# First expert products in split f16, denominators by half as many columns, one transpose and six expert products moved, a residual addition on GpSimd

## Chip, cores and metric

The kernel runs on one core of one Trainium2 chip, as one program. The metric is the device time of one execution in microseconds (us); a kernel is given as the median of its executions. TensorE (matrix products; PE in the profile, PEld its weight loads), VectorE (DVE), ScalarE (ACT), GpSimd (POOL) and the DMA queue of SyncE (SP) run side by side, each through its own list of instructions, and wait for one another on semaphores.

## What is computed

Two layers over x (16 batches, 56 rows, 128 wide). Each layer is a cross attention to a context of 1500 keys per batch, then a mixture of 8 experts of which each row takes 2. Both are scaled by tanh of a gain and added to x. Layer 1 has a key mask and a shared expert. The reference, shortened:

```python
def xattn(q_in, ctx, mask):            # H = 16 heads of 8
    q, k, v = heads(q_in @ Wq + bq), heads(ctx @ Wk + bk), heads(ctx @ Wv + bv)
    w = softmax(where(mask == 0, -1e9, q @ k.T / sqrt(8)))   # layer 0: no mask
    return join(w @ v) @ Wo + bo
def ffn0(x):                           # layer 0: 8 experts, 128 -> 512 -> 128
    p = softmax(x @ gate_w); top2 = top_k(p, 2), divided by their sum
    h = gelu(x @ w1[e] + b1[e]); y = h @ w2[e] + b2[e]
    return sum over the two of share * y
def ffn1(x):                           # layer 1: sigmoid gate, 128 -> 64 -> 128, and a shared expert
    ...
x = x + tanh(g_xattn[l]) * xattn(layernorm(x), ctx, mask)
x = x + tanh(g_ffn[l]) * ffn(layernorm(x))
```

## The kernel before

Everything is f32 unless it is said otherwise. A "batch" n is one of 32 (layer, batch) pairs; two batches side by side (T = 112 rows) form a group, for which queries, attention output and experts are computed together. The program is a software pipeline written out by hand: steps s = -1 to 35, each of 12 sub-steps kt = 0 to 11. Step s works on several batches at once:

- keys of batch s + 1 and values of batch s are projected (`project`, L1265 and L1274; f16 operands, each split in a high and a low part, three products);
- TensorE computes scores of batch s once to find their maxima (`max_scores`, L1229, two chunks of 500 keys in each sub-step, into the two halves of pMX; VectorE reduces each in `largest`, L1072). The next chunk but one waits for that reduction;
- scores of batch s - 1 (from sub-step 3) and s - 2 (up to sub-step 2) are computed again, shifted by the maximum (`score_half`, L1187), ScalarE takes the exponential (L789), and every other sub-step (the even ones) TensorE multiplies by the values (`weigh`, L1208, f32, into pO);
- odd steps from 3 have the first part of the experts of a group (`has_a`), even steps from 4 the second (`has_f`), odd steps from 5 the end (`has_end`).

The order of the small pieces within a step stands in tables: `kv_uses` (the projections in pKV), `fh_uses` (buffer pFH) and `fy_uses` (buffer pFY). An entry (kt, name, n) says that TensorE does the piece at the end of sub-step kt, and VectorE reads the result at the start of the next. pFH and pFY are single buffers: each piece waits until VectorE has read the one before it (`free`). The maximum reductions of a sub-step stand behind those reads in VectorE's list.

The names that matter here:

- **h0 to h7** in pFH (L1399): first product of expert e of layer 0, 4 f32 matmuls of 128x128 by 112 columns (each two instructions in the trace). VectorE adds the bias and writes HR (`hidden`, L970), ScalarE applies Gelu in sub-step 9 of the even step (L798). h0, h1 are at sub-steps 10, 11 of the odd step, h2 to h7 at 0 to 5 of the even one. There are 8 such groups, with their even steps 4 to 18; in steps 16 and 18 the attention is already that of layer 1.
- **ct** in pFY (L1306): the maxima (`m`, then `cc`, L1082 to L1087) are transposed and copied to ct (L1010), from where SyncE sends them as two shift rows into qexp (L546). `score_half` of batch s - 1 waits for that DMA at sub-step 3.
- **sum** (L1287): VectorE masks pO into OM (L1098), both heads of a pair in columns of their own (224); a product with sel gives the denominators, VectorE takes the reciprocal rden (L1014), GpSimd multiplies OM by it (L688) and adds the value bias into ON (L689). **y** (L1293) is the output projection, 4 f32 matmuls.
- **xT** (L1297, L1027): normalized rows of the group, transposed, in f32 as xnfT. **y0 to y3**: second expert products (L1328 and L1332), weighted by the shares in VectorE (L1043), added up on GpSimd (L709 to L714). **yb** (L1039): the expert biases and the residual input.
- VectorE ends the group in sub-step 11 of the odd step: X = acc1 * gain + acc0 (L1122). In its list, the maxima m and cc of the next step come right behind it.
- GpSimd splits the next context into Chi and Clo (L730, L732), and the keys into khi and klo (L641, L643).

In layer 0 the maximum products and the scores use different row halves of TensorE's array, and run side by side (`together`); in layer 1 they use all rows (`apart_`).

## Time and profile before

| | us |
|---|---|
| median of three runs | 1011.62 (1010.51 to 1013.26) |
| the profiled execution: its time | 1013.23 |
| the profiled execution: its span | 1011.4 |
| TensorE busy | 899.4 (89%), mean granted clock 0.97 |
| VectorE busy | 730.1 (72%) |
| ScalarE busy | 588.1 (58%) |
| GpSimd busy | 516.9 (51%) |

The page of the profile gives busy times, the span in 40 slices, the chain that ended last and the costliest groups of instructions. The view by line groups the instructions of a line by shape: count, busy time, mean ns, and what ended the idle time before them. The view in order of time shows start, duration, engine and line, with the idle time in brackets. Durations of matmuls contain their latency: what one costs in a stream is read from the start of the next.

### The profile page before, as it was taken

The numbers are of one execution on the slowest core, as the hardware profiler recorded it, in microseconds if no ns is written. First come the engines' busy times: TensorE is split into PE (matmuls) and PEld (weight loads), VectorE is DVE, ScalarE is ACT, GpSimd is POOL, SyncE is SP. The second block draws the span as 40 slices with busy tenths as digits, with TensorE's granted clock in tenths as the row PEclk, the third lists the DMA queues.
The fourth block names the chain that finished last, engine by engine and source line by source line (L and its number), as shares of the span: only waits on it lengthen the run. The fifth ranks groups of instructions, "written<-read, shape, count | busy, mean of one in ns | idle before, by whom it ended". The sixth has DMA issues, their size and how long they took to land.

```text
span 1011.4 us, 32583 instructions
## 1 busy us (share of the span) xinstructions
PE 899.4 (89%) x13088; PEld 651.2 (64%) x13088; DVE 730.1 (72%) x1576; ACT 588.1 (58%) x1077; POOL 516.9 (51%) x662
## 2 busy tenths in 40 slices
PE   3888998989899898988999999999999899999975
PEld 1355676766767676776767776666666666666754
DVE  5675876868678587786867858777787778787723
ACT  2155666575755757557475575757666575757560
POOL 5544554545445354553555456676666576662211
PEclk9978999999999999999999999999999999999995
DMA  6245432212222122222656656676766656675200
GB/s 158 77 123 150 129 112 92 80 49 73 70 84 78 51 68 72 80 79 67 119 116 127 138 96 142 137 156 127 156 148 121 140 124 143 137 137 99 55 2 19
DMA packets 103554, 104.47 MB, mean 103 GB/s; under 512 B 28442, under 2 KB 97388, under 8 KB 103404
## 3 DMA queue, kind: packets, MB, share of 16 engines
q1 hardware_dynamic: 101986, 102.07, 43.3%
q8 instruction: 104, 1.70, 0.8%
q10 hardware_dynamic: 1418, 0.32, 0.2%
q14 instruction: 46, 0.38, 0.1%
HBM read 35.89 MB, written 0.46 MB: 36 GB/s over the span
## 4 chain that ended last, share of the span: by engine, by line
PE 58%; DVE 25%; ACT 9%; issue 6%; DMA 1%; ACTq 1%; SPq 0%; DVEq 0%
DVE mx L1072 14%; PE pO L1208 13%; PE pMX L1229 10%; PE pST L1187 8%; PE pKV L1274 6%; PE pKV L1265 6%; PE pFH L1399 5%; PE pFY L1328 3%; ACT P L789 2%; DVE rden L1014 2%; ACT HR L798 2%; DVE HR L970 2%; ACT L789 2%; PE pFY L1332 2%; DVE ysc L1043 1%
## 5 line engine op out<-in xcount | busy, mean ns | idle before, releaser
L1072 DVE TENSOR_REDUCE mx<-pMX 112x1 f32<-112x500 f32 x768 | 487.4, 668 | 127.9 <-PE pMX L1229 125.0
L789 ACT ACTIVATE P<-pST 125x448 f32<-125x448 f32 x768 | 389.6, 542 | 277.7 <-PE pST L1187 272.4
L1229 PE MATMUL pMX<-kop,qmax 48*112 48x500 f16 (+1 forms) x768 | 284.3, 408 | 50.1 <-DVE mx L1072 37.3
L1187 PE MATMUL pST<-qexp,kop 50*128 50x112 f16 (+2 forms) x3072 | 266.7, 215 | 13.0 <-ACT P L789 7.9
L1187 PEld LDWEIGHTS pST<-qexp,kop 50*128 50x128 f16 (+2 forms) x3072 | 183.7, 100 | 78.0 <-issue 23.8
L1208 PE MATMUL pO<-P,V 125*17 125x112 f32 x6144 | 188.5, 264 | 0.0
L1229 PEld LDWEIGHTS pMX<-kop,qmax 48*112 48x112 f16 (+1 forms) x768 | 97.4, 129 | 124.0 <-DVE mx L1072 57.6
L1208 PEld LDWEIGHTS pO<-P,V 125*17 125x17 f32 x6144 | 138.1, 98 | 35.0 <-issue 18.7
L641 POOL CAST khi<-kfull 128x500 f16<-128x500 f32 x96 | 57.7, 601 | 190.1 <-ACT kfull L816 188.6
L643 POOL TENSOR_TENSOR klo<-kfull,khi 128x500 f16<-128x500 f32 x96 | 108.8, 1134 | 7.8
L732 POOL TENSOR_TENSOR Clo<-C,Chi 128x500 f16<-128x500 f32 x93 | 105.7, 1137 | 7.5
L821 ACT ACTIVATE V<-pKV 125x512 f32<-125x512 f32 x96 | 57.0, 594 | 36.9 <-PE pKV L1274 32.8
L688 POOL TENSOR_TENSOR OM<-OM,rden 128x224 f32<-128x224 f32 x32 | 21.0, 657 | 106.7 <-DVE rden L1014 106.7
L1399 PE MATMUL pFH<-xnfT,w1a 128*128 128x112 f32 x512 | 70.9, 281 | 5.0 <-DVE HR L970 4.9
L816 ACT ACTIVATE kfull<-pKV,bkp 128x500 f32<-128x500 f32 x48 | 32.5, 677 | 69.2 <-PE pKV L1265 65.9
L1274 PE MATMUL pKV<-Whi,Chi 128*128 128x128 f16 (+1 forms) x384 | 72.1, 225 | 0.5
L1274 PE MATMUL pKV<-Whi,Clo 128*128 128x128 f16 (+1 forms) x384 | 71.4, 223 | 0.4 <-issue 0.4
L1274 PE MATMUL pKV<-Wlo,Chi 128*128 128x128 f16 (+1 forms) x384 | 71.4, 223 | 0.0
L1399 PEld LDWEIGHTS pFH<-xnfT,w1a 128*128 128x128 f32 x512 | 63.6, 191 | 11.3 <-DVE HR L970 8.9
L1043 DVE TENSOR_TENSOR ysc<-pFY,gate 112x512 f32<-112x512 f32 x32 | 22.1, 691 | 61.5 <-PE pFY L1328 45.0
L730 POOL CAST Chi<-C 128x500 f16<-128x500 f32 x93 | 56.5, 607 | 17.6 <-PE pKV L1274 14.7
L1328 PE MATMUL pFY<-w2a,HR 128*112 128x128 f32 x512 | 61.1, 275 | 3.6 <-ACT HR L798 3.6
(151 smaller groups left out, 1106.8 us busy)
## 6 DMA issues: line engine op xcount, KB each, us to landing
C<-in_ctxT SPq DMA_DIRECT2D x31, 750.0 KB, 6.7
kop<-maskop SPq DMA_DIRECT2D x48, 437.5 KB
kop<-khi SPq DMA_DIRECT2D x192, 62.5 KB
kop<-khi SPq DMA_DIRECT2D x96, 125.0 KB
kop<-klo SPq DMA_DIRECT2D x96, 62.5 KB
kop<-klo SPq DMA_DIRECT2D x48, 125.0 KB
maskin<-in_mask SPq DMA_DIRECT2D x8, 656.2 KB, 5.5
qexp<-qmax SPq DMA_DIRECT2D x16, 182.0 KB
```

The source lines that it names most:

```text
L641: nc.gpsimd.tensor_copy(khi[:, cols], kfull[:, c, :]).then_inc(khi_done, 1)
L643: nc.gpsimd.tensor_tensor(klo[:, cols], kfull[:, c, :], khi[:, cols], ALU.subtract).then_inc(klo_done, 1)
L732: nc.gpsimd.tensor_tensor(Clo[:, s % 2, cols], C[:, cols], Chi[:, s % 2, cols], ALU.subtract).then_inc(ctx_split, 1)
L789: nc.scalar.activation(P[0:KP, slot, h * 4 * T:(h + 1) * 4 * T], pST[0:KP, h, 0:4 * T], ACT.Exp, scale=EXP_SCALE).then_inc(exp_done, 1)
L1072: nc.vector.tensor_reduce(mx[:, s % 2, c, p:p + 1], pMX[0:T, m % 2, 0:CW], AX.X, ALU.max).then_inc(max_done, 1)
L1187: mm = nc.tensor.matmul(pST[0:keys.stop - keys.start, h, i * T:(i + 1) * T], kop[rows, b, slot, keys], qexp[rows, b, slot, :, :].rearrange ...
L1208: mm = nc.tensor.matmul(pO[32 * g:32 * g + VW, r * T:(r + 1) * T], V[0:KP, b, tile, p, :], P[0:KP, tile % RING, p * T:(p + 1) * T], start= ...
L1229: nc.tensor.matmul(pMX[0:T, m % 2, 0:CW], qmax[rows, b, slot, :, :].rearrange("r j q -> r (j q)"), kop[rows, b, slot, c * CW:(c + 1) * CW] ...
L1265: mm = nc.tensor.matmul(pKV[:, 0:CW], m[:, l, 0, :], x_[:, b, cols], start=(i == 0), stop=(i == 2))
L1274: mm = nc.tensor.matmul(pKV[0:rows, i * D:(i + 1) * D], x_[:, s % 2, cols], m[:, l, 1, :], start=(k == 0), stop=(k == 2))
L1328: mm = nc.tensor.matmul(o, HR[:, F0C * e + c, :], w2a[:, e, c, :], start=(c == 0), stop=(c == F0C - 1))
L1399: mm = nc.tensor.matmul(pFH[:, c * T:(c + 1) * T], w1a[:, e, c * 128:(c + 1) * 128], xnfT[:, :], start=True, stop=True)
```

## The change

1. w1 of layer 0 is kept as two f16 tensors w1hi and w1lo, and xT also writes f16 parts xfhi and xflo. Each f32 product of h0 to h7 becomes three f16 products (hi hi, hi lo, lo hi). The raw weights pass through the buffer HR. ScalarE makes w1hi (8 copies in steps 2 and 3), GpSimd w1lo (8 subtractions), and one of the eight loads moves from step 2 to step 3.
2. Masking pO becomes two instructions that bring both heads of a pair into the same 112 columns of OM. V has one more column of ones. The products of sum, the reciprocal, and OM and ON on GpSimd have half as many columns, and y has two matmuls instead of four. The tensors bvm and the wide headmask go away.
3. ct is transposed in the middle of sub-step 1, behind the first half of the scores, instead of at the end of sub-step 0; VectorE copies it between the two maxima of sub-step 1.
4. h2 to h7 are at sub-steps 0, 1, 2, 3, 6, 7 instead of 0 to 5.
5. X is made on GpSimd in two instructions (multiply, add) behind its sums, in all groups but the last.

The diff, cut to its core:

```diff
-VW = PR + 1
+VW = PR + 2
@@ fh_uses / fy_uses
-        uses += [(e - 2, f"h{e}", 1) for e in range(2, 8)]
+        uses += [(k, f"h{e}", 1) for e, k in zip(range(2, 8), (0, 1, 2, 3, 6, 7))]
-        uses.append((0, "ct", 1))
+        uses.append((1, "ct", 1))
@@ SyncE, expert_weights
-                if s in (1, 2):
-                    for e in range(4 * (s - 1), 4 * s):
-                        sp.dma_start(w1a[:, e, :], w1_0[e]).then_inc(w1_in[e // 2], 16)
+                if s in (1, 2, 3):
+                    for e in range(4 * (s - 1), min(4 * s, E0 - 1)) if s < 3 else (E0 - 1,):
+                        if e == E0 - 1:
+                            sp.wait_ge(w1_split, 1)
+                        sp.dma_start(w1raw[:, raw_columns(e)], w1_0[e]).then_inc(w1_in[e], 16)
@@ GpSimd
+            def expert_low(st, i):
+                if st.s in (2, 3):
+                    e = 4 * (st.s - 2) + i
+                    pool.wait_ge(w1_hi, e + 1)
+                    nc.gpsimd.tensor_tensor(w1lo[:, e, :], w1raw[:, raw_columns(e)], w1hi[:, e, :], ALU.subtract
+                                            ).then_inc(w1_split, 1)
                 low_part(st, 0)
+                expert_low(st, 0)
...
                 low_part(st, 1)
+                expert_low(st, 1)
...
                 low_part(st, 2)
+                expert_low(st, 2)
+                expert_low(st, 3)
...
                     nc.gpsimd.tensor_tensor(acc[:, 1, :], ysc[:, 0, 0, :], ysc[:, 0, 1, :], ALU.add).then_inc(ysum_done, 1)
+                    pool.wait_ge(ysum_done, end_count(s) + 1)
+                    link(nc.gpsimd.tensor_scalar(acc[:, 1, :], acc[:, 1, :], gains[0:T, g:g + 1], None, ALU.mult))
+                    pool.wait_ge(fy_free, upto(fy_uses, s, "yb", True))
+                    nc.gpsimd.tensor_tensor(xg((s - 5) // 2), acc[:, 1, :], acc[:, 0, :], ALU.add).then_inc(x_done, 1)
@@ ScalarE
+                    if s in (2, 3) and kt in (1, 3, 5, 7):
+                        e = 4 * (s - 2) + kt // 2
+                        act.wait_ge(w1_in[e], 16)
+                        nc.scalar.activation(w1hi[:, e, :], w1raw[:, raw_columns(e)], ACT.Copy).then_inc(w1_hi, 1)
@@ VectorE
-                        nc.vector.reciprocal(rden[:, :], pFY[:, 0:2 * T]).then_inc(fy_free, 1)
+                        nc.vector.reciprocal(rden[:, :], pFY[:, 0:T]).then_inc(fy_free, 1)
-                        nc.vector.tensor_copy(xnfT[:, :], pFY[:, 0:T]).then_inc(fy_free, 1)
+                        if l == 0:
+                            link(nc.vector.tensor_copy(xnfT[:, :], pFY[:, 0:T]))
+                            link(nc.vector.tensor_copy(xfhi[:, :], pFY[:, 0:T]))
+                            nc.vector.tensor_tensor(xflo[:, :], pFY[:, 0:T], xfhi[:, :], ALU.subtract).then_inc(fy_free, 1)
+                        else:
+                            nc.vector.tensor_copy(xnfT[:, :], pFY[:, 0:T]).then_inc(fy_free, 1)
-                        nc.vector.tensor_tensor(OM[:, s % 2, :], pO[:, 0:2 * T],
-                                                headmask[:, :, :, :].rearrange("p r j q -> p (r j q)"),
-                                                ALU.mult).then_inc(o_free, 1)
+                        link(nc.vector.tensor_scalar(om, of[:, 0], headmask[:, 0:1], None, ALU.mult))
+                        nc.vector.scalar_tensor_tensor(out=om, in0=of[:, 1], scalar=headmask[:, 1:2], in1=om,
+                                                       op0=ALU.mult, op1=ALU.add).then_inc(o_free, 1)
+                    if kt == 1 and has_m(s - 1):
+                        from_fy(0, "ct")
-                    if has_end(s) and kt == 11:
-                        if not ends(s):
-                            dve.wait_ge(ysum_done, end_count(s) + 1)
+                    if ends(s) and kt == 11:
@@ TensorE
-                        mm = nc.tensor.matmul(pFY[:, 0:2 * T], sel[:, :], OM[:, s % 2, :], start=True, stop=True)
+                        mm = nc.tensor.matmul(pFY[:, 0:T], sel[:, :], OM[:, s % 2, :], start=True, stop=True)
-                            for j in range(2):
-                                mm = nc.tensor.matmul(pFY[0:T, 0:D], ON[:, r, j, :, :].rearrange("p b q -> p (b q)"), woE[:, l, r, :],
-                                                      start=(r == 0 and j == 0), stop=(r == 1 and j == 1))
+                            mm = nc.tensor.matmul(pFY[0:T, 0:D], ON[:, r, :, :].rearrange("p b q -> p (b q)"), woE[:, l, r, :],
+                                                  start=(r == 0), stop=(r == 1))
                             score_half(st, kt, h)
+                            if kt == 1 and h == 0 and has_m(s - 1):
+                                small("ct")
...
                         score_half(st, kt, 0)
+                        if kt == 1 and has_m(s - 1):
+                            small("ct")
-                                    mm = nc.tensor.matmul(pFH[:, c * T:(c + 1) * T], w1a[:, e, c * 128:(c + 1) * 128],
-                                                          xnfT[:, :], start=True, stop=True)
+                                    for i, (w1, x_) in enumerate(((w1hi, xfhi), (w1hi, xflo), (w1lo, xfhi))):
+                                        mm = nc.tensor.matmul(pFH[:, c * T:(c + 1) * T], w1[:, e, c * 128:(c + 1) * 128],
+                                                              x_[:, :], start=(i == 0), stop=(i == 2))
```

## Rows read from the trace of the kernel before

**Rows 1.** The page: busy time, share of the span and instructions of each engine.

```profile
PE 899.4 (89%) x13088; PEld 651.2 (64%) x13088; DVE 730.1 (72%) x1576; ACT 588.1 (58%) x1077; POOL 516.9 (51%) x662
```

**Rows 2.** Stretch, length, PE PEld DVE ACT POOL busy, granted clock, DMA share, GB/s.

```profile
216.73:278.33 61.60, 55.71 (x872) 43.31 (x869) 46.09 (x98) 37.32 (x68) 29.18 (x39) 1.00 0.22 70
480.00:600.00 120.00, 115.17 (x1619) 86.24 (x1611) 86.74 (x183) 72.06 (x128) 66.49 (x78) 1.00 0.62 119
764.00:766.00 2.00, 2.00 (x32) 1.34 (x25) 0.84 (x3) 0.41 (x1) 1.21 (x2) 0.50 1.04 134
```

**Rows 3.** By line and shape: count, busy us, mean ns, idle time before them.

```profile
L1399 PE MATMUL pFH<-xnfT,w1a 128*128 128x112 f32 x512 | 70.9, 281 | 5.0 <-DVE HR L970 4.9
L1274 PEld LDWEIGHTS pKV<-Whi,Clo 128*128 128x128 f16 (+1 forms) x384 | 39.6, 103 | 0.0
L1014 DVE RECIPROCAL rden<-pFY 128x224 f32<-128x224 f32 x32 | 49.4, 1544 | 2.2 <-PE pFY L1287 2.2
L1054 DVE RECIPROCAL g<-g 112x8 f32<-112x8 f32 x8 | 1.6, 203 | 0.3
```

**Rows 4.** TensorE in order of time, step 8 (layer 0).

```profile
249.15 1.15 PE L1399 MATMUL pFH<-xnfT,w1a 128*128 128x112 f32 x8 [0.23 <-DVE HR L970]
250.22 0.42 PE L1229 MATMUL pMX<-kop,qmax 48*112 48x500 f16 x1
254.20 1.04 PE L1399 MATMUL pFH<-xnfT,w1a 128*128 128x112 f32 x8
255.17 0.41 PE L1229 MATMUL pMX<-kop,qmax 48*112 48x500 f16 x1
```

**Rows 5.** TensorE in order of time: first and last of twelve f16 value products.

```profile
300.75 0.23 PE L1274 MATMUL pKV<-Whi,Chi 128*128 128x128 f16 x1
...
301.38 0.22 PE L1274 MATMUL pKV<-Whi,Clo 128*128 128x128 f16 x1
```

**Rows 6.** VectorE in order of time, end of step 7 and start of step 8.

```profile
245.05 0.62 DVE L970 TENSOR_TENSOR HR<-pFH,W 128x448 f32<-128x448 f32 x1 [0.43 <-PE pFH L1399]
246.76 1.11 DVE L1122 SCALAR_TENSOR_TENSOR X<-acc,gains 112x128 f32<-112x128 f32 x1
247.79 0.17 DVE L1082 TENSOR_REDUCE m<-mx 112x8 f32<-112x24 f32 x1
248.00 0.36 DVE L1086 TENSOR_SCALAR cc<-m 112x8 f16<-112x8 f32 x1
252.26 0.63 DVE L970 TENSOR_TENSOR HR<-pFH,W 128x448 f32<-128x448 f32 x1
```

**Rows 7.** GpSimd in order of time, same place as rows 6.

```profile
246.59 1.14 POOL L732 TENSOR_TENSOR Clo<-C,Chi 128x500 f16<-128x500 f32 x1
```

**Rows 8.** VectorE in order of time, steps 3 and 4, where no X is made.

```profile
122.73 0.62 DVE L970 TENSOR_TENSOR HR<-pFH,W 128x448 f32<-128x448 f32 x1 [0.43 <-PE pFH L1399]
129.07 0.62 DVE L970 TENSOR_TENSOR HR<-pFH,W 128x448 f32<-128x448 f32 x1
```

**Rows 9.** Both engines in order of time, step 7, sub-steps 1 and 5.

```profile
219.64 1.24 DVE L1072 TENSOR_REDUCE mx<-pMX 112x1 f32<-112x500 f32 x2
220.00 2.00 PE L1328 MATMUL pFY<-w2a,HR 128*112 128x128 f32 x16
231.10 0.37 DVE L1098 TENSOR_TENSOR OM<-pO,headmask 128x224 f32<-128x224 f32 x1
235.39 0.70 DVE L996 TENSOR_SCALAR qhi<-pFH,head_of 128x112 f16<-128x112 f32 x2 [0.17 <-PE pFH L1390]
```

**Rows 10.** VectorE in order of time, layer 1, the same place as rows 6.

```profile
793.61 0.69 DVE L1122 SCALAR_TENSOR_TENSOR X<-acc,gains 112x128 f32<-112x128 f32 x1
794.42 0.97 DVE L1086 TENSOR_SCALAR cc<-m 112x8 f16<-112x8 f32 x1
```

**Rows 11.** The chain that ended last, in order of time: start, us, what.

```profile
980.81 1.57 DVE rden L1014
986.67 2.06 PE pFY L1293 x8
```

More of the change, by code:

```diff
@@ L217, in links @@
         n += 2
+    if is_batch(s - 2):
+        n += 1
     if has_q(s):
@@ L365, in build @@
         xnfT = sb("xnfT", [128, T])
-        ones = xnfT
+        xfhi, xflo = sb("xfhi", [128, T], F16), sb("xflo", [128, T], F16)
         lg = sb("lg", [T, NE])
@@ L392, in build @@
         w_in, x_in, f_in, f2_in, wo_in = sem("w_in"), sem("x_in"), sem("f_in"), sem("f2_in"), sem("wo_in")
-        w1_in, w2_in = [sem(f"w1_in{i}") for i in range(4)], [sem(f"w2_in{i}") for i in range(4)]
+        w1_in, w2_in = [sem(f"w1_in{i}") for i in range(E0)], [sem(f"w2_in{i}") for i in range(4)]
         c_in = sem("c_in")
@@ L427, in build @@
         gelu_done = sem("gelu_done")
+        w1_hi, w1_split = sem("w1_hi"), sem("w1_split")
         x_done = sem("x_done")
@@ L930, in output_biases @@
                 dve.wait_ge(init_a, 1)
-                dve.wait_ge(init_l, 7)
-                for j in range(2):
-                    for l in range(LAYERS):
-                        for r in range(2):
-                            nc.vector.tensor_scalar(bvm[:, l, r, j, :], ones[:, 0:S], rowmask[:, j:j + 1],
-                                                    bvE[:, l, r:r + 1], ALU.mult, ALU.mult).then_inc(init_l, 1)
+                dve.wait_ge(init_l, 6)
                 for l in range(LAYERS):
@@ L1042, in from_fy @@
                         k = int(use[1]) // 2
+                        if k == 0 and end_count(s - back):
+                            dve.wait_ge(ysum_done, end_count(s - back))
                         nc.vector.tensor_tensor(ysc[:, k, :, :], pFY[0:T, 0:4 * D].rearrange("t (e d) -> t e d", e=4),
@@ L1077, in step @@
                 for kt in range(KT):
+                    if s == 3 and kt == 11:
+                        dve.wait_ge(w1_split, E0)
                     if s == 1 and kt == 8:
@@ L1370, in step @@
                         score_half(st, kt, 1)
-                    for use in [u[1] for u in fy_uses(s) if u[0] == kt and not early(u[1])]:
+                    for use in [u[1] for u in fy_uses(s) if u[0] == kt and u[1] != "ct" and not early(u[1])]:
                         small(use)
```

65 lines of the change are left out of this document (37 added, 28 removed).

## The prediction

> **What bounds the kernel now.** I read the engines' shares first: TensorE is busy 89% of the span, VectorE 72% [rows 1]. A share is a mean, so I went on to busy time by stretch [rows 2]: a pair of steps of layer 0 takes 61.60 us with TensorE busy for 55.71, steps 16 to 18 have it busy for 115.17 of 120.00, and layer 1 for 326.29 of 350.00. TensorE sets the pace, but not everywhere. The order of time shows where VectorE does: in the light sub-steps (no `weigh`, no projection) it has two maxima (1.17 us from start to start) and the bias of one expert (0.54 us), and TensorE waits for it before the next expert, 0.23 us in the row of 249.15 [rows 4]. From h0's bias at 245.05 to h3's at 252.26 VectorE is busy nearly throughout [rows 6]. In heavy sub-steps TensorE is late and VectorE idles. So a shorter TensorE piece counts in full in a heavy sub-step and hardly in a light one, and a shorter VectorE piece the other way round.
>
> **The change part by part.** I make the sum per kind of step, by walking both engines through the twelve sub-steps with the durations of the rows.
>
> *Expert products.* One expert costs 1.07 us from its start to the next maximum's after a wait and 0.97 us in a stream [rows 4]. As f16 it is twelve products of 112 columns. The nearest rows are the value products, f16 with 128 columns: 0.63 us for eleven intervals, 0.057 us each [rows 5]. Twelve are 0.68 us at that rate and 0.60 if the time goes with the columns; I take 0.65. One expert saves 0.3 to 0.45 us, I take 0.38, and 64 experts take 24 us off TensorE.
>
> *X off VectorE.* It holds VectorE for 1.03 us at 246.76 (to the start of m at 247.79) [rows 6]. Steps 3 and 4, which make no X, show its worth in the old kernel: from h0's bias to h3's take 6.34 us there and 7.21 us in step 7 [rows 6, 8], so 0.87 us. But it is long because GpSimd runs at the same time: it ends when Clo (246.59 + 1.14) ends [rows 7], and cc, 0.36 us here, takes 0.97 us in layer 1 [rows 6, 10]. Without X, cc comes earlier, into the stream of Chi and Clo, which the two new GpSimd instructions (about 1.3 us) push later. I charge 0.3 us; the bounds are 0 and 0.8. The Trainium skill (GPSIMD Engine Reference, Specifications) says that GpSimd shares its SBUF interfaces with VectorE, with contention for VectorE instructions in a 2-port mode or with two SBUF inputs; the trace agrees, as X and cc are the ones that stretch.
>
> *Even step of layer 0.* From h0's bias to sub-step 2: X gone -1.03, h0 and h1 sooner -0.35, the rest of the experts' saving hidden behind VectorE, ct no longer waiting for cc -0.55, cc in contention +0.3: -1.65. Sub-steps 2 to 7: h4 and h5 leave their places and h6 and h7 come to 6 and 7, where VectorE has time since rden shrinks. rden is 1.54 us for 224 columns and 0.20 for 8 [rows 3], so 0.85 for 112: -0.70. TensorE now paces this stretch: four experts -1.4 and the half sum product -0.2, against +0.35 for the masking in two instructions and +0.2 for tighter waits on the single buffer: -1.05. Together -2.7 (bounds -1.5 and -4.0, the latter eight experts at 0.38 and X in full). The later ct still has time: its DMA is issued at sub-step 1 and needed at 3.
>
> Steps 6, 8, 10, 12, 14: 5 x 2.7 = 13.5. Step 4 has no X to lose: 2.7 - 1.0 = 1.7. Steps 16 and 18 are TensorE's nearly alone [rows 2]: eight experts at 0.38 and part of X and rden, 3.5 each, 7.0.
>
> *Odd steps get longer.* (a) y2 is now behind ct in the single buffer pFY, so it waits for VectorE's copy, which stands between the maxima of sub-step 1. Those start at 219.64, y2 at 220.00 [rows 9]; the copy would end at 220.35. That is +0.35, and nothing behind y2 takes it back, since TensorE is late there. (b) The masking of pO takes two instructions. The nearest pair, also linked by a wait, is qhi, 0.70 us for two [rows 9], against 0.30 from OM's start to the next maximum's: +0.35, and sum and both maxima of sub-step 5 stand behind it. (c) Half the sum product gives back 0.1. The reciprocal and y give nothing, since from qhi at 235.39 [rows 9] up to xT VectorE has no gap, and rden lies ahead of that, beside TensorE's heavy sub-step. xT's two further instructions (0.65 us) lie in sub-step 10, where VectorE idled for 0.76 us; if that cover went, they would cost up to 0.65. So +0.6 in each of 7 steps (5 to 17): +4.2.
>
> *Layer 1.* Even steps: X and the wait for cc -0.6, rden on VectorE's run behind sum -0.7, masking +0.35, half a sum product -0.05: -1.0, 6 times (20 to 30), -6.0. Odd steps, 19 to 31: +0.45 as above, 7 times, +3.2. y saves 0.5 us of TensorE, but the next maximum waits for VectorE there.
>
> *Start.* ScalarE's 8 copies (some 0.6 us) and GpSimd's 8 subtractions (1.13 us, as klo) lie in steps 2 and 3. Behind GpSimd's last two stand xnf and the context split of step 3. SyncE's new wait for w1_split is over a step before; behind it stand the context load and the key DMAs. I take +1.0 (bounds 0 and +4). Masking twice +0.7, rden in step 2 -0.7: +1.0 in all.
>
> *End.* rden, 1.57 us, and y, 2.06 us at half the clock, lie bare on the chain [rows 11]: -0.7 and -1.0. Masking +0.35, sum -0.2, and ct later by 0.45 in step 32, where its DMA was waited for: -1.1.
>
> Sum: +1.0 - 1.7 - 13.5 - 7.0 + 4.2 - 6.0 + 3.2 - 1.1 = -20.9 us. On the profiled execution, 1013.23 us with a span of 1011.4, that is 992.3; the median of the runs, 1011.62, is 1.6 lower than that execution, so **990.7, say 991 us**.
>
> **The rivals.** *TensorE alone decides* (B): all 24 us of the experts count, with X at 0.87 in 13 steps (11), rden and y as above (8), and the odd steps' charges are half absorbed (-4): about -36, **976 us**. For it speaks the 89% of rows 1, against it the wait in rows 4.
>
> *VectorE and GpSimd get in each other's way* (C): cc and X's successors cost the upper bound, 0.8, not 0.3, in 13 steps (+6.5), and the light sub-steps hide more (1.0 less in each of 6 even steps, +6): -8.4, **1003 us**, range 998 to 1010. For it speaks the 0.97 us of rows 10.
>
> *The clock falls* (D), a case on the other side: layer 0's TensorE has 55.71 busy in 61.60 us at the full granted clock, 1.00 [rows 2]; the change takes about 4 us of work from it and 2 us from the time. In layer 1 there is a stretch at 0.50, the lower level (1.2 GHz), from 764 on [rows 2]. If 3 us of TensorE's work run at half the clock, they take 1.5 us more. From 14 such stretches on, one for each step of layer 0 from 4 on, the gain is gone: 991 + 21 = **1012 us**. Against it: the pair of layer 0 leaves TensorE idle a tenth of the time already, and stays at 1.00 throughout.
>
> *The f16 products don't stream* (E), slower: their f16 weight load lasts 103 ns [rows 3]. If each product waited for its own, an expert would take 12 x 0.103 = 1.24 us instead of 1.07 at most: +0.17 x 64 = +11, in place of the 15 us that experts give in the sum (1.5 in each of 6 steps, 3.0 in each of 2): -20.9 + 15 + 11 = +5, **1017 us**. It decides from 0.09 us a product. Rows 5 speak against it, 0.057 us with the same loads. The Trainium skill (TensorE: Matmul & The Clock Gate, Back-to-back issue gap) gives about 81 ns for a product of 128 columns in a stream of loads and products; by that an expert would take 0.97 us and save nothing in a stream. The trace disagrees at 57 ns.
>
> **How the numbers follow.** Forecast 0.52, B 0.12, C 0.26, D 0.06, E 0.04. The forecast's own bounds are 984 to 998. The range, 978 to 1004, takes in C's middle and the near side of B and leaves out the rest of them, D and E. A measurement of this kernel can tell about 0.3%, 3 us. Faster: forecast, B and nearly all of C, 0.88; same 0.05 (the end of C, part of D); slower 0.07.
>
> **What would show it.** An expert of twelve f16 products should take 0.60 to 0.68 us; rden 0.85 us; a pair of steps of layer 0 about 59.5 us instead of 61.6, with VectorE without a gap from h0's bias to sub-step 2, and h0's bias to h3's in 5.7 to 6.2 us instead of 7.21. y2 in odd steps should wait for ct, and sum for OM longer than before. cc's duration tells forecast from C, granted clocks below 1.00 in layer 0 tell D. The forecast is wrong if GpSimd's new instructions delay the context split up to the projections, if ScalarE's exponentials come late in the shorter even steps, or if the shift rows' DMA is waited for at sub-step 3 in more steps than 32.

## The result, and the profile after

The changed kernel takes 1021.51 us (1018.42 to 1024.61), the one before 1011.07 beside it: a ratio of 1.010, 95% interval 1.0065 to 1.0134. It is slower; 991 was forecast, with 978 to 1004 as the range. The profiled execution takes 1018.42 us with a span of 1016.4, against 1013.23 and 1011.4 before, so the two traces show 5.0 us of the difference. A kernel's time below is the median of its executions, without those that are over 1.5% above its fastest, which count as slow (one each of e5, e9, e10 and e13; the profile of e13 is of that one). First the page of the changed kernel, its span and its engines (busy us, share, instructions):

```profile
span 1016.4 us, 33063 instructions
PE 884.0 (87%) x13280; PEld 628.1 (62%) x13280; DVE 720.5 (71%) x1600; ACT 593.1 (58%) x1085; POOL 526.5 (52%) x701
```

TensorE and VectorE both have less to do than before [rows 1], and the program is longer. Where the time went I read from the starts of each step's first maximum reduction. "Undisturbed" are steps in which TensorE's granted clock stays at 1.00:

| us | before | after | change | forecast |
|---|---|---|---|---|
| start up to step 4 | 125.66 | 127.48 | +1.8 | +1.0 |
| step 4 | 31.09 | 29.41 | -1.7 | -1.7 |
| even steps 6 to 14, each | 30.92 | 29.40 | -1.5 | -2.7 |
| odd steps 5 to 15, each undisturbed | 30.67 | 30.90 | +0.2 | +0.6 |
| steps 16; 18 | 34.20; 32.24 | 33.39; 31.14 | -0.8; -1.1 | -3.5 each |
| even steps of layer 1, each (20 to 28 but 24) | 26.40 | 27.17 | +0.8 | -1.0 |
| odd steps of layer 1, each undisturbed | 29.20 | 29.35 | +0.15 | +0.45 |
| from the start of step 31 | 78.34 | 77.04 | -1.3 | -0.65 (-1.1, and +0.45 for step 31) |
| stretches at half clock in steps 5 to 15 | 0 | 11.2 | +11.2 | 0 |

The last line is what four odd steps take over 30.90: step 5 34.16, step 9 33.63, step 11 32.77, step 13 34.19. Steps 17 and 19 stand in no row: +0.15 (32.41, now 32.56) and +0.7 (31.08, now 31.77); step 24 takes 26.29, and "How long cc is held" comes back to it. Windows of the changed kernel (start:end, length, then busy time and instructions of PE, PEld, DVE, ACT, POOL, the granted clock, DMA share, GB/s): an undisturbed pair of steps (7 and 8), step 5's two stretches, and all of steps 4 to 15.

```profile
220.44:280.75 60.31, 53.10 (x900) 40.00 (x902) 45.71 (x102) 37.56 (x68) 29.30 (x41) 1.00 0.23 72
171.00:173.00 2.00, 1.78 (x24) 1.11 (x28) 2.00 (x4) 0.89 (x3) 0.75 (x2) 0.71 0.31 122
173.00:175.00 2.00, 2.00 (x30) 1.09 (x23) 0.80 (x2) 0.28 (x1) 0.76 (x2) 0.50 0.19 63
178.00:180.00 2.00, 1.69 (x26) 1.25 (x30) 1.79 (x7) 1.09 (x2) 0.30 (x1) 0.67 0.07 14
180.00:182.00 2.00, 2.00 (x35) 1.62 (x25) 1.03 (x2) 0.00 (x0) 1.60 (x4) 0.50 0.13 27
127.48:500.45 372.97, 329.55 (x5388) 247.44 (x5380) 275.22 (x602) 226.36 (x405) 180.25 (x248) 0.97 0.26 77
```

The pair takes 60.31 us where before took 61.60 [rows 2]; forecast was 59.5. In step 5 the clock falls to 0.50 (1.2 GHz) twice, each time for 3.4 us, and TensorE is then busy throughout: at half speed it works off what stands in those sub-steps. Before, layer 0 had none from step 4 on.

The second thing to see is cc. VectorE's list at the step's end, in order of time (start, duration, engine, line, operation, operands), and below it GpSimd's over the same time:

```profile
247.54 0.62 DVE L997 TENSOR_TENSOR HR<-pFH,W 128x448 f32<-128x448 f32 x1
248.08 1.25 DVE L1108 TENSOR_REDUCE mx<-pMX 112x1 f32<-112x500 f32 x2
249.36 0.18 DVE L1120 TENSOR_REDUCE m<-mx 112x8 f32<-112x24 f32 x1
249.58 0.77 DVE L1124 TENSOR_SCALAR cc<-m 112x8 f16<-112x8 f32 x1
250.38 0.51 DVE L1125 SCALAR_TENSOR_TENSOR cc<-cc,m 112x8 f16<-112x8 f16 x1
250.81 0.61 DVE L997 TENSOR_TENSOR HR<-pFH,W 128x448 f32<-128x448 f32 x1
...
254.34 0.60 DVE L997 TENSOR_TENSOR HR<-pFH,W 128x448 f32<-128x448 f32 x1
```

```profile
248.10 0.46 POOL L745 TENSOR_TENSOR X<-acc 112x128 f32<-112x128 f32 x1 [0.21 <-POOL acc L742]
248.50 0.60 POOL L761 CAST Chi<-C 128x500 f16<-128x500 f32 x1
249.18 1.14 POOL L763 TENSOR_TENSOR Clo<-C,Chi 128x500 f16<-128x500 f32 x1
250.26 0.60 POOL L761 CAST Chi<-C 128x500 f16<-128x500 f32 x1
```

X has left VectorE. But cc's first instruction, on 8 columns, takes 0.77 us and ends at 250.35; Clo beside it ends at 250.32. The second takes 0.51 and ends at 250.89; Chi ends at 250.86. Before, X ended with Clo in the same manner [rows 6, 7]. From h0's bias to h1's it is 3.27 us now and was 3.42 (245.05 to 248.47): of X's 1.03 us 0.15 were gained.

The steps of the forecast that can be read directly: an expert takes 0.69 us, from its first product after the wait to the next maximum's; y2 waits for ct; sum waits longer for OM (before 0.38 us); rden takes 0.85. Four rows of TensorE and one of VectorE, in the order of the sentence, the first two for the expert:

```profile
251.48 0.22 PE L1445 MATMUL pFH<-xfhi,w1hi 128*128 128x112 f16 x1 [0.79 <-DVE HR L997]
252.17 0.42 PE L1271 MATMUL pMX<-kop,qmax 48*112 48x500 f16 x1
222.53 1.67 PE L1369 MATMUL pFY<-w2a,HR 128*112 128x128 f32 x13 [0.36 <-DVE ct L1037]
234.46 0.45 PE L1329 MATMUL pFY<-OM,sel 128*128 128x112 f32 x2 [0.69 <-DVE OM L1140]
235.40 0.85 DVE L1041 RECIPROCAL rden<-pFY 128x112 f32<-128x112 f32 x1
```

### The profile page after: what moved, and what is told of

Its sections match the earlier page's. It is cut to its first block, busy times and chain, and to the rows that moved or that the text cites. A ratio compares the mean times of both kernels' runs of the same rounds, so it can differ in the third digit from the quotient of the medians.

```text
span 1016.4 us, 33063 instructions
## 1 busy us (share of the span) xinstructions
PE 884.0 (87%) x13280; PEld 628.1 (62%) x13280; DVE 720.5 (71%) x1600; ACT 593.1 (58%) x1085; POOL 526.5 (52%) x701
## 4 chain that ended last, share of the span: by engine, by line
PE 56%; DVE 26%; ACT 10%; issue 6%; DMA 1%; ACTq 1%; SPq 0%; DVEq 0%
DVE mx L1108 14%; PE pO L1250 14%; PE pMX L1271 10%; PE pST L1229 8%; PE pKV L1307 7%; PE pKV L1316 6%; PE pFY L1369 3%; ACT P L820 3%; PE pFH L1445 2%; ACT HR L829 2%; ACT L820 2%; DVE HR L997 2%; PE pFY L1373 2%; DVE ysc L1079 1%; DVE cc L1124 1%
## 5 line engine op out<-in xcount | busy, mean ns | idle before, releaser
L1271 PE MATMUL pMX<-kop,qmax 48*112 48x500 f16 (+1 forms) x768 | 292.2, 412 | 57.3 <-DVE mx L1108 45.3
L1229 PE MATMUL pST<-qexp,kop 50*128 50x112 f16 (+2 forms) x3072 | 271.8, 216 | 15.8 <-ACT P L820 11.4
L1229 PEld LDWEIGHTS pST<-qexp,kop 50*128 50x128 f16 (+2 forms) x3072 | 186.0, 101 | 80.5 <-ACT P L820 25.1
L1250 PE MATMUL pO<-P,V 125*18 125x112 f32 x6144 | 192.1, 267 | 0.0
L1250 PEld LDWEIGHTS pO<-P,V 125*18 125x18 f32 x6144 | 140.7, 100 | 35.1 <-issue 16.5
L1369 PEld LDWEIGHTS pFY<-w2a,HR 128*112 128x112 f32 x512 | 59.3, 181 | 10.6 <-issue 5.8
L711 POOL TENSOR_TENSOR OM<-OM,rden 128x112 f32<-128x112 f32 x32 | 13.5, 423 | 87.4 <-DVE rden L1041 87.4
L687 POOL TENSOR_SCALAR veq<-mvq 112x1 f32<-112x1 f32 x16 | 3.6, 227 | 89.8 <-DVE mvq L1178 89.8
```

The source lines that it names most:

```text
L1229: mm = nc.tensor.matmul(pST[0:keys.stop - keys.start, h, i * T:(i + 1) * T], kop[rows, b, slot, keys], qexp[rows, b, slot, :, :].rearrange ...
L1250: mm = nc.tensor.matmul(pO[32 * g:32 * g + VW, r * T:(r + 1) * T], V[0:KP, b, tile, p, :], P[0:KP, tile % RING, p * T:(p + 1) * T], start= ...
L1271: nc.tensor.matmul(pMX[0:T, m % 2, 0:CW], qmax[rows, b, slot, :, :].rearrange("r j q -> r (j q)"), kop[rows, b, slot, c * CW:(c + 1) * CW] ...
L1369: mm = nc.tensor.matmul(o, HR[:, F0C * e + c, :], w2a[:, e, c, :], start=(c == 0), stop=(c == F0C - 1))
```

## The experiments

Theory 1 is the clock (the prediction's D): TensorE has less to do in places, its clock falls, and that takes the gain. Theory 2 is VectorE and GpSimd in each other's way (C). The parts are numbered as in "The change".

**Parts undone one at a time.** Part 5 undone, X back on VectorE (e2):

```diff
-                    nc.gpsimd.tensor_tensor(xg((s - 5) // 2), acc[:, 1, :], acc[:, 0, :], ALU.add).then_inc(x_done, 1)
...
-                    if ends(s) and kt == 11:
+                    if has_end(s) and kt == 11:
+                        if not ends(s):
+                            dve.wait_ge(ysum_done, end_count(s) + 1)
```

> The changed kernel with X made on VectorE again (part 5 undone). The prediction charged cc 0.3 us for GpSimd's company and counted the leaving of X as 1.03 us in even steps of layer 0 and 0.6 in layer 1: by it this kernel is slower than the changed one by 5 x 0.75 + 2 x 0.5 + 6 x 0.6 = about 8 us. Theory 2 (contention): the two cc instructions take 1.3 to 1.6 us together behind GpSimd's X and split, against 0.53 behind VectorE's own X, so X on GpSimd gives nothing: this kernel takes the same time or up to 3 us less, and cc is back at 0.36 and 0.17 us in even steps of layer 0. Theory 1 says nothing of it beyond stretches that stay as they are.

1028.47 us, ratio to before 1.0163 (1.0123 to 1.0203): 7 us slower than the changed kernel. So X on GpSimd is a gain, near the 8 us that follow from the prediction, but not by its mechanism. The steps show half: odd steps go from 30.90 to 31.16 (layer 0) and from 29.35 to 29.67 (layer 1), even steps stay at 29.41 and 27.11, some 3.5 us; the rest is left to the stretches, which I can't assign for each execution. cc was not back at 0.36. VectorE, then GpSimd:

```profile
254.22 0.55 DVE L1159 SCALAR_TENSOR_TENSOR X<-acc,gains 112x128 f32<-112x128 f32 x1
254.69 0.17 DVE L1113 TENSOR_REDUCE m<-mx 112x8 f32<-112x24 f32 x1
254.90 0.98 DVE L1117 TENSOR_SCALAR cc<-m 112x8 f16<-112x8 f32 x1
255.91 0.17 DVE L1118 SCALAR_TENSOR_TENSOR cc<-cc,m 112x8 f16<-112x8 f16 x1
```

```profile
254.71 1.14 POOL L756 TENSOR_TENSOR Clo<-C,Chi 128x500 f16<-128x500 f32 x1
```

Now cc ends with Clo again, 255.88 and 255.85. X, which here has Clo only behind it, holds VectorE for 0.47 us (254.22 to the start of m at 254.69) where it was 1.03 [rows 6]. In these rows whichever of X and cc stands beside Clo ends with it, so a little over half of X's 1.03 us, 0.56, was this wait.

Part 3 undone, ct back at sub-step 0 (e3, and a second time as e16):

```diff
-        uses.append((1, "ct", 1))
+        uses.append((0, "ct", 1))
...
-                            if kt == 1 and h == 0 and has_m(s - 1):
-                                small("ct")
```

> The changed kernel with the shift rows transposed at the end of sub-step 0 again (part 3 undone). By the prediction this takes 0.35 us off each of 14 odd steps (y2 no longer waits for the copy) and puts 0.55 on each of 13 even steps (the copy waits for cc): +2 us. If cc's 1.4 us in company is the case, ct comes later by another 0.9 us and this costs up to 0.9 more in each even step and in layer 1's odd steps: +8 to +14 us.

1007.96 us (0.9982; 0.9952 to 1.0013), 13 us faster than the changed kernel. Both expectations had it slower. Odd steps of layer 0 go from 30.90 to 30.46, as the 0.36 us wait of y2 says; even steps stay at 29.41 to the hundredth. The 0.55 us that the late ct was to save there doesn't exist in the changed kernel. The step lengths give some 4 of the 13 us. The rest is left to the stretches: its profile has none in sub-steps 5 and 7, and three at the starts of odd steps.

Part 2 undone, the wide denominators (e4, and again as e17):

```diff
-                        link(nc.vector.tensor_scalar(om, of[:, 0], headmask[:, 0:1], None, ALU.mult))
-                        nc.vector.scalar_tensor_tensor(out=om, in0=of[:, 1], scalar=headmask[:, 1:2], in1=om,
-                                                       op0=ALU.mult, op1=ALU.add).then_inc(o_free, 1)
+                        nc.vector.tensor_tensor(OM[:, s % 2, :], pO[:, 0:2 * T],
+                                                headmask[:, :, :, :].rearrange("p r j q -> p (r j q)"),
+                                                ALU.mult).then_inc(o_free, 1)
...
-                        nc.vector.reciprocal(rden[:, :], pFY[:, 0:T]).then_inc(fy_free, 1)
+                        nc.vector.reciprocal(rden[:, :], pFY[:, 0:2 * T]).then_inc(fy_free, 1)
```

> The changed kernel with the wide denominators again (part 2 undone: masking in one instruction, rden 1.54 us, four f32 products in y, 224 columns in sum). Theory 1: TensorE's load in sub-steps 5 to 8 is back, so the half-clock stretches of odd steps go as in e1_fill, 8 to 12 us; the rest comes out even (masking -0.3, rden +0.7 where it had been given back anyway): about 1010. Theory 2: the narrower rden is a gain kept on VectorE, so undoing it costs: 0.7 us in the even steps, about 1021.5 + 13 x 0.4 = 1027.

1010.36 us (0.9975; 0.9956 to 0.9995), 11 us faster. The compact form is worth 0.42 us in an even step of layer 0 and costs 0.33 in an odd one, 0.3 to 0.7 in steps 16 to 18, and 0.8 in an even step of layer 1 (27.17 to 26.37). That is some 6 of the 11 us; the rest is again left to the stretches.

Part 1 undone, h0 to h7 as f32 products (e5, and again as e13), and part 4 undone, h2 to h7 in sub-steps 0 to 5 (e6):

```diff
-                                    for i, (w1, x_) in enumerate(((w1hi, xfhi), (w1hi, xflo), (w1lo, xfhi))):
-                                        mm = nc.tensor.matmul(pFH[:, c * T:(c + 1) * T], w1[:, e, c * 128:(c + 1) * 128],
-                                                              x_[:, :], start=(i == 0), stop=(i == 2))
+                                    mm = nc.tensor.matmul(pFH[:, c * T:(c + 1) * T], w1a[:, e, c * 128:(c + 1) * 128],
+                                                          xnfT[:, :], start=True, stop=True)
```

```diff
-        uses += [(k, f"h{e}", 1) for e, k in zip(range(2, 8), (0, 1, 2, 3, 6, 7))]
+        uses += [(e - 2, f"h{e}", 1) for e in range(2, 8)]
```

> The changed kernel with h0 to h7 as f32 products again (part 1 undone). An expert's start-to-start cost goes back from 0.69 to about 1.0 us, 64 of them. Prediction's step: the f16 experts carry 15 us of its sum, so undoing them costs 12 to 18 us if the clock stays: 1034 to 1039. Theory 1 (clock): the longer products also fill sub-steps 6 and 7 and 10 and 11, the half-clock stretches get fewer, and 5 to 8 us come back: 1026 to 1031. If even steps of layer 0 are set by something else than the experts they stay near 29.4 us and the undoing costs under 5.

> The changed kernel with h2 to h7 in sub-steps 0 to 5 again (part 4 undone). If VectorE bounds sub-steps 1 to 5 of the even step, as the prediction has it, the two biases (0.54 us each) come back onto its path: an even step of layer 0 goes from 29.4 to 29.9 to 30.4 us, 4 to 8 us in all. If TensorE sets the even step's 29.4 us the placing is nearly free: within 1 us a step either way, 1019 to 1023.

e5: 1018.50 us (1.0102; 1.0049 to 1.0154), from three executions at 1018.37, 1018.50 and 1028.02. Even steps of layer 0 go to 30.49 (+1.1), step 16 to 37.35 (+4.0), step 18 to 33.16 (+2.0). Step 16 has a stretch at half clock in e5 and none in the changed kernel; the same stretch made e14's step 16, below, 1.6 us longer, so the experts' part of the 4.0 is some 2.4, an estimate. 6 x 1.1 + 2.4 + 2.0 = 11 us for the f16 experts, against the 15 of the sum. Yet the kernel is no slower than the changed one: its profile had no stretch in steps 5 to 15. That looked like theory 1 with the experts as its cause. e6: 1022.24 us (1.0111; 1.0089 to 1.0133), even steps 29.70 (+0.3) but step 16 32.75 (-0.6): the places are nearly free, the lower of the two cases.

**Is it TensorE's lack of work?** e1 gives back part 2's TensorE work alone; e9 issues some maximum products twice, where TensorE waits.

```diff
+                        nc.tensor.matmul(pFY[:, T:2 * T], sel[:, :], OM[:, s % 2, :], start=True, stop=True)
...
+                        for r in range(2):
+                            nc.tensor.matmul(pFY[0:T, D:2 * D], ON[:, r, :, :].rearrange("p b q -> p (b q)"),
+                                             woE[:, l, r, :], start=True, stop=True)
```

```diff
+                twice = {1: (6, 7, 8, 9, 10, 11, 14, 15, 22), 0: (18, 19, 22)}
+                if 4 <= n <= 18 and layer_of(n) == 0 and m in twice[n % 2]:
+                    nc.tensor.matmul(pMX[0:T, m % 2, 0:CW], qmax[rows, b, slot, :, :].rearrange("r j q -> r (j q)"),
+                                     kop[rows, b, slot, c * CW:(c + 1) * CW], start=True, stop=True)
```

> The changed kernel with TensorE's old load given back: two more f32 products stand ahead of y and one of 112 columns ahead of sum, both into columns of the buffer that nobody reads. Nothing else moves. Theory 1 (clock): the stretches at half the granted clock in odd steps of layer 0 start because sum and y no longer fill sub-steps 5 to 8. Then most of the stretches near 80, 172, 180, 360 and 422 us go, steps 5, 9, 11 and 13 fall from 33 to 34 us to about 31, the mean granted clock rises from 0.96 to about 0.97, and the time falls from 1021.5 by 8 to 12, to about 1011, although TensorE has 0.6 us more to do in each step pair. Theory 2 (the two vector engines in each other's way): the clock is a bystander, the time stays or rises by the products' cost, 1021 to 1025.

> The changed kernel; in layer 0, steps 4 to 15, some of the maximum products are issued twice into the same buffer (0.21 us each), where TensorE waits for VectorE anyway: odd steps in sub-steps 3, 4, 5, 7 (both chunks) and 11 (the first), even steps in 9 (both) and 11 (the first). Theory 1 (clock): these waits (0.85, 0.53, 0.45 and 0.92 us of idle TensorE in sub-steps 3, 4, 5 and 7) are what the stretches at half clock follow. With them filled the stretches of layer 0 from step 4 on go and 9 to 12 us come back: 1009 to 1013, with the undisturbed steps still at 29.4 and 30.9 us. Rival (the stretches depend on when the steps fall, not on what TensorE does there): as many stretches at other places, 1019 to 1024, or longer by the added products.

e1: 1016.05 us (1.0058; 1.0032 to 1.0083). Added work makes it 5 us faster, with undisturbed steps unchanged at 29.41 and 30.89. Its profile has one stretch in sub-steps 5 and 7 of odd steps, where the changed kernel's first has five and its second (e14, below) two. e9: 1018.77 us (1.0052; 1.0025 to 1.0078), and its profile has 27 us at half clock in steps 5 to 15, as much as the changed kernel's 24. That profile is of the longest of nine executions (1013.30 to 1023.67), and against the kernel before e9 comes out as e1 does. Nor are the waits filled: TensorE's idle time in sub-steps 4 to 7 of an undisturbed odd step goes from 2.0 us to 1.5 (1.4 in e1), in sub-step 7 from 0.92 to 0.82 (0.59 in e1). So e9 misses its forecast, but it settles nothing for or against theory 1.

**Parts together.** e7 undoes parts 2 and 3, e8 parts 2, 3 and 5 (the edits above).

> Parts 2 and 3 undone together: f16 experts, their places and X on GpSimd stay. The two single undoings took 6 and 3.5 us off the step lengths outside of half-clock stretches. Were these separate causes they add: a pair of steps of layer 0 takes 59.9 to 60.0 us (60.3 in the changed kernel, 61.6 before), a pair of layer 1 55.4 to 55.6, and the time is 1001 to 1004. If both had the same cause (the single buffer and the masking in front of sub-step 5 delaying the same maxima), it stays at 1006 to 1008.

> Parts 2, 3 and 5 undone: only the f16 experts and their places stay. By e2_x_vector, X on VectorE costs 0.26 us in each odd step of layer 0 and 0.3 in each of layer 1: 3 to 4 us over e7, 1005 to 1008. If X on GpSimd pays only in the company of the other parts (contention with the two added GpSimd instructions is gone here), the two are equal.

e7: 1004.95 us (0.9939; 0.9917 to 0.9961), faster than both kernels. Its undisturbed pair:

```profile
219.42:279.39 59.97, 54.03 (x904) 40.38 (x906) 46.70 (x99) 37.55 (x68) 30.19 (x41) 1.00 0.23 72
279.00:281.00 2.00, 2.00 (x42) 1.63 (x44) 1.70 (x6) 0.96 (x2) 0.00 (x0) 0.64 0.34 110
```

In the step lengths the gains of the two undoings add: an odd step of layer 0 takes 30.15 (30.90 - 0.44 - 0.33 = 30.13), a pair of layer 1 55.25. In the times they don't: 17 us together, where 13 and 11 had come singly, since either alone already takes the stretches in sub-steps 5 and 7 away. The second row is the start of one of its four stretches, at the start of step 9: step 9 takes 31.42, so here a stretch costs 1.27 us. e8: 1009.31 us (0.9979; 0.9961 to 0.9997), 4 us over e7. Part 5 is worth that much here: 0.34 in each odd step of layer 1 (29.19 and 28.85), and in layer 0 each of the six odd steps of e8's profile has a stretch, where e7's has four.

**How long cc is held.** In e4 cc took 0.46 us at the start of layer 1's odd steps, in the changed kernel 1.07, in the kernel before 0.40 to 0.44. The spare GpSimd product in e11 and e12 moves GpSimd's stream and gives neither VectorE nor TensorE anything to do:

```diff
+                    link(nc.gpsimd.tensor_tensor(spare[:, :], OM[:, s % 2, :], rden[:, :], ALU.mult))
```

> The changed kernel with one more GpSimd product of 112 columns (about 0.45 us, into a spare tile) between OM and ON, so that GpSimd's stream stands where it stood with the wide denominators; VectorE and TensorE have nothing more. Theory 2 (cc is held until the GpSimd instruction beside it ends): in layer 1 cc's first instruction at the start of odd steps falls from 1.07 to about 0.45 us as in e4, an even step of layer 1 from 27.2 to about 26.5 us, 3 to 4 us in all; in layer 0 nothing changes. If cc's duration has another cause, nothing changes or the step grows with the later GpSimd work: 1021 to 1025.

> The changed kernel with two spare GpSimd products between OM and ON. In e11 the one product (0.50 us) fell into 0.45 us in which GpSimd waited for keys anyway, so its later instructions stood where they were. The second moves them by 0.45 to 0.5 us. Theory 2 (cc is held until the GpSimd instruction that runs beside it ends): in even steps of layer 1 the last Clo but not Chi now stands behind cc; cc's first instruction at the start of odd steps falls from 1.07 to 0.2 to 0.5 us and those even steps from 27.18 to 26.4 to 26.6 us. Rival: cc stays at 1.0 us or over and the steps at 27.2 us.

e11: 1021.16 us (1.0073; 1.0046 to 1.0100), cc 1.08: a miss, since the product went into a gap. In the changed kernel khi stood behind 0.45 us of idle time; in e11 there is none (GpSimd of the changed kernel, then of e11):

```profile
643.03 0.37 POOL L712 TENSOR_TENSOR ON<-OM,bvE 128x112 f32<-128x112 f32 x1
643.85 0.60 POOL L653 CAST khi<-kfull 128x500 f16<-128x500 f32 x1 [0.45 <-ACT kfull L847]
```

```profile
648.36 0.42 POOL L713 TENSOR_TENSOR spare<-OM,rden 128x112 f32<-128x112 f32 x1
648.87 0.37 POOL L714 TENSOR_TENSOR ON<-OM,bvE 128x112 f32<-128x112 f32 x1
649.19 0.60 POOL L654 CAST khi<-kfull 128x500 f16<-128x500 f32 x1
```

e12, with two: 1012.97 us (1.0038; 1.0017 to 1.0059). More GpSimd work, and 8.5 us faster. cc beside GpSimd, in the changed kernel and in e12:

```profile
655.28 1.07 DVE L1124 TENSOR_SCALAR cc<-m 112x8 f16<-112x8 f32 x1
...
655.20 1.13 POOL L763 TENSOR_TENSOR Clo<-C,Chi 128x500 f16<-128x500 f32 x1
```

```profile
652.38 0.34 DVE L1127 TENSOR_SCALAR cc<-m 112x8 f16<-112x8 f32 x1
...
652.09 0.60 POOL L764 CAST Chi<-C 128x500 f16<-128x500 f32 x1
```

In the one cc meets Clo and ends with it (656.35 and 656.33), in the other Chi (652.72 and 652.69). The kernel before had it as in e12 (VectorE, then GpSimd):

```profile
651.19 0.40 DVE L1086 TENSOR_SCALAR cc<-m 112x8 f16<-112x8 f32 x1
...
650.96 0.60 POOL L730 CAST Chi<-C 128x500 f16<-128x500 f32 x1
```

The changed kernel has a case of its own: behind step 24 cc comes as Chi ends (768.35 against 768.48) and takes 0.17, and step 24 is 26.29 us long, not 27.17. Even steps of layer 1 fall from 27.18 to 26.45, odd ones rise by 0.27: 2 us in the two kinds together. Between the two profiled executions (1018.4 and 1012.3) another 1.3 us lie ahead of step 4 and 3.1 in stretches, of which e12 has fewer; why is open. The Trainium skill (SBUF — State Buffer, Who interferes with whom) says that VectorE in a 2-port mode contends with GpSimd for the port pair they share, and that whichever issues first has it for the whole instruction while the other is blocked. The trace agrees in this: cc ends with the GpSimd instruction that started before it, Clo or Chi. That cc runs in such a mode no run shows.

**Which kernels have the stretches.** One profile of a kernel shows one execution, and the stretches vary between executions. Four kernels have a second one.

> The kernel of e5 (changed kernel, f32 experts) a second time, for its stretches at half clock: e5's profile had none in layer 0 from step 4 to 15. If f32 experts keep the clock up, this profile has none there either, or one at most, and the fast executions lie within a few us of 1018; if e5 was chance, it has three or more stretches like the changed kernel.

> The changed kernel a second time, for its stretches: the first profile had seven of 3.4 us or twice that in steps 5 to 13, worth 11 us. If the stretches belong to the kernel, this one has as many, though perhaps in other odd steps, and undisturbed steps of 29.4, 30.9, 27.2 and 29.35 us; if they were chance, it has few and the execution takes about 1010.

> The kernel of e3 a second time. With the compact denominators TensorE idles 2.0 us in sub-steps 4 to 7 of an odd step of layer 0 (1.1 with the wide ones), with ct early or late. Seven profiles of kernels with the compact denominators and the late ct have 24 stretches that start in sub-steps 5 and 7 of steps 5 to 15; e3, with the early ct, had none. If the idle time alone starts them, this profile has two or more there, and e3 was chance; if the late ct is needed too, it has none again, and the time is 1007 to 1009.

> The kernel of e4 a second time: wide denominators, late ct, idle time in sub-steps 4 to 7 of 1.1 us. e4's profile had no stretch starting in sub-steps 5 and 7 of steps 5 to 15, and three at the starts of steps 5, 9 and 15. Expected again: none in sub-steps 5 and 7, two to four at the starts of odd steps (they come with the f16 experts: none in the three profiles of layer 0 with f32 experts), 1008 to 1012.

e13: 1021.46 us (1.0125; 1.0064 to 1.0186); its executions lie between 1017.31 and 1033.90, and the profile is of the longest. It has eight stretches in sub-steps 5 and 7 of steps 5, 7, 9 and 11, 3.3 us in each of these steps. So this kernel has such stretches in some executions, and e5's profile without one was not the rule. That f32 experts do nothing for the clock isn't shown: the step lengths are 11 us longer, and yet the three executions each of e5 and e13 that count have a mean of 1022.2, the eight of the changed kernel and e14 one of 1021.5. By these numbers the f32 form loses less to the stretches on average. Two windows of e13:

```profile
174.00:176.00 2.00, 2.00 (x36) 1.35 (x34) 1.49 (x3) 0.68 (x2) 0.79 (x2) 0.50 0.10 32
182.00:184.00 2.00, 2.00 (x30) 1.45 (x19) 0.81 (x2) 0.00 (x0) 1.67 (x4) 0.50 0.15 34
```

e14: 1022.44 us (1.0113; 1.0082 to 1.0144), undisturbed steps as in the first profile, four stretches in steps 5, 7 and 9. e16: 1009.63 us (0.9976; 0.9954 to 0.9998), none in sub-steps 5 and 7. e17: 1009.77 us (0.9968; 0.9948 to 0.9989), none either. Stretches that begin in steps 5 to 15 of each profile, counted in the windows of half a microsecond:

| kernels (profiles) | in sub-steps 5 to 7 of odd steps | at the start of an odd step |
|---|---|---|
| compact and late ct: the changed kernel, e14, e1, e2, e5, e6, e9, e11, e12, e13 (10) | 36 (28 without e13) | 13 |
| one or both undone: before, e3, e4, e7, e8, e10, e15 to e18 (10) | 0 | 24 |
| of both groups, with f32 experts: before, e5, e13 (3) | 8 | 0 |

(Two counts in the expectations were off: e16's 24 in seven profiles is 36 in ten, and the changed kernel's first profile has six stretches in these steps, not seven.) One stretch of e16, in step 12, stands in neither column. The first kind came only with parts 2 and 3 together: TensorE's idle time in sub-steps 4 to 7 is 2.0 us with the compact denominators and 1.1 without, but e3 and e16 have the 2.0 as well and no such stretch. What in the two parts starts it is open. Undoing either also changes the length of a pair of steps (60.31, in e3 59.87, in e4 60.40), and no run keeps TensorE's waits and shifts the steps alone, so e9's rival, that it depends on when the steps fall, stands. A pair of the first kind in one step costs 3.3 us. The second kind showed up only with f16 experts (none in three profiles without) and costs 1.3 us with the early ct, 2.7 with the late one, where it lasts twice as long.

**Against the second kind**, in e7's kernel: maximum products issued twice in odd and even steps (e10), in odd ones only (e15), in even ones only (e18).

```diff
+                twice = {1: (6, 7, 10, 14, 15, 22, 23), 0: (10, 12, 13, 18, 19, 22)}
```

> The kernel of e7 with maximum products issued twice in the same way: odd steps in sub-steps 3 and 7, 11 (both chunks) and 5 (one), even steps in 6 and 9 (both), 5 and 11 (one). e7 had four stretches of 3.4 us at half clock at the starts of steps 9, 11, 13 and 15, each worth 1.27 us. Theory 1: they go, 4 to 6 us: 999 to 1001. Rival: they stay, 1004 to 1007.

> The kernel of e10 with the doubled maximum products of its odd steps only (sub-steps 3, 5, 7, 11). The stretches of e7 began at the start of odd steps, behind the waits in sub-steps 9 to 11 of the even step. If those waits in the even step are what counts, the stretches at the starts of odd steps are back: 1004 to 1006. If the waits in odd steps count too, or the step lengths alone, there are none, the even steps are back at 29.83, and the time is 1001 to 1003.

> The kernel of e7 with the doubled maximum products of the even steps only (sub-steps 5, 6, 9, 11), the complement of e15. The stretches of e7 start at the start of an odd step, right behind these waits. e15, which fills the odd steps only, had one such stretch instead of four. If filling near them works as well or better, there are none or one here and the time is 1001 to 1003; if only the odd steps' waits count, three or four stay: 1005 to 1007, with even steps 0.13 us longer in either case.

e10: 1002.14 us (0.9894; 0.9861 to 0.9927), no stretch in steps 5 to 15, even steps 0.13 us longer. e15: 1001.22 us (0.9916; 0.9888 to 0.9945), one. e18: 1003.87 us (0.9894; 0.9851 to 0.9936), three, at the starts of steps 11, 13 and 15. The profiles point at the waits in the odd steps, though the stretch comes 30 to 50 us behind them, and not at the ones right in front of it. But they are single profiles with 0, 1 and 3 stretches where e7 had 4, and the times don't bear the order out: against the kernel before, e18 is as fast as e10 and no slower than e15, and one execution of e18 took 997.90. All three lie under e7's 0.9939, with intervals that overlap its own. Steps 4 to 15 of e15, with the clock at 1.00, against 0.97 in the changed kernel above:

```profile
129.03:490.51 361.48, 330.83 (x5456) 246.31 (x5447) 280.41 (x591) 226.37 (x405) 185.50 (x248) 1.00 0.27 80
```

e10, e15 and e18 can't be told apart by their times. e15 has the lowest median, 20 us under the changed kernel, and is 0.8% under the kernel before, some 9 us. It keeps parts 1, 4 and 5.

## Why the prediction was wrong

On the profiled executions 992.3 was forecast and 1018.4 came: 26 us. By the table above the undisturbed steps make 17 of them and the clock 9 (11.2 in layer 0 and 1.6 in layer 1, less 3.6 that the kernel before had in its steps 21 and 25). Without the stretches from step 4 on, the two executions would be 1005.6 and 1009.6, by an estimate from these numbers: of a forecast gain of 21 us the step lengths left 4, and the clock turned that into a loss.

*Expert products.* Right in size: 0.69 us, saving 0.28 to 0.38 of the 0.97 to 1.07 before [rows 4], and some 11 us by e5 where the sum had 15. E is out.

*X off VectorE* (-1.03, with +0.3 for cc) is the first step that failed. Of X's 1.03 us 0.56 was a wait for GpSimd's Clo, and here that wait didn't go with the instruction that bore it: cc took it over, 0.77 and 0.51 us for 0.36 and 0.17. h0's bias to h3's takes 6.80 us, not 5.7 to 6.2. This is C's mechanism, and the two cc's together take 0.75 us more, C's 0.8 and not the 0.3 of the sum. The 0.97 us that spoke for C [rows 10] were no usual row of layer 1, though: they stand behind step 25 with its stretch, and at the ten other starts of steps 20 to 30 cc took 0.36 to 0.44. e7 and e8 put part 5 at 0.34 us in each odd step of layer 1.

*ct not waiting for cc* (-0.55) is worth nothing: e3's even steps are the same to 0.01 us. The cost was seen and right: +0.43 us at y2.

*rden in even steps* kept its 0.70 only until TensorE was late; e4 puts the whole of part 2 at -0.42 there. In odd steps rden gave nothing, as said, and the masking cost 0.30 (0.35).

*Steps 16 and 18* (-3.5 each, -0.8 and -1.1 came). The experts gave some 2.4 and 2.0 there (e5, the first without its stretch), but the new places cost 0.6 and 0.2 (e6), the compact masking 0.3 and 0.7 (e4). That makes -1.5 and -1.1; of the rest in step 16 no run tells.

*Layer 1, even* (-1.0; +0.8 came) is the largest miss of the undisturbed steps, 9 us in six. The sum had X, rden and cc as gains. What came was a GpSimd stream that stood 0.4 us earlier in the step than with the wide denominators (e4), with shorter OM and ON, so that cc met Clo and not Chi: +0.6. e12 moves it back and the steps are at 26.45. A faster GpSimd was nowhere in the sum.

*The clock* (D, 1012 at a chance of 0.06). The argument against it was that layer 0 idles a tenth of the time already and stays at 1.00. That says what the old arrangement of waits did, nothing of a new one. D's price of 1.5 us a stretch was near (1.3 to 2.7), its count of 14 too high: six in steps 5 to 15 and one in step 29. That the clock takes the time is shown; why it falls is open. D and C came together, which the list of rivals, one at a time, did not allow for; they hold 6 and 26% of the chance. (B's terms add up to -39, not -36; nothing hangs on it.)

## What to carry to other kernels

If two engines share a path, the duration of a short instruction may be the rest of another engine's long one: look whether both end together before counting it as a gain. And a shorter piece on a third engine changes which instruction meets which. On a kernel near TensorE's limit, undo parts singly even when each looks harmless: here undoing one or the other of two parts of five gives 11 and 13 us, both together 17, and the three others alone make it faster than before. For a clock that falls in some steps, compare undisturbed steps first and count the falls in several profiles; one profile without any meant little (e5), and neither did one of the longest execution (e9).

## What the runs showed of the hardware

Added work made the kernel faster: idle GpSimd products by 8.5 us (e12), of which the steps that it shortens explain 2, and unread TensorE products by 5.5 (e1). Doubled ones in e7's kernel gave 0.2 to 0.5% (e10, e15, e18), which the intervals don't settle. TensorE's granted clock fell to 0.50 (1.2 GHz) in 74 stretches of 3.4 or 6.8 us in steps 5 to 15 of the 20 profiles, although TensorE was busy for 2.9 to 3.7 of the 4 us ahead of each, and no single gap in them was longer than 0.92 us. A VectorE instruction on 8 columns takes 0.17 us alone and up to 1.09 beside GpSimd.
